# Gated slot attention and fp8 feed-forward: keys times queries with tokens in partitions, softmax weights turned by VectorE and DRAM

## The chip, the cores and the metric

The kernel runs on one core of a Trainium2 chip. The metric is the device time of one execution in microseconds (us). TensorE (PE in the profile) multiplies matrices; its weight loads are shown apart as PEld. VectorE (DVE), ScalarE (ACT) and GpSimd (POOL) work on vectors, and SyncE (SP) issues the DMAs. Each engine takes its instructions in program order and waits on semaphores that others raise.

## What is computed

Four batches of 512 tokens with 512 features go through a layer norm, an attention with 16 heads and 64 memory slots per head, a residual, another layer norm and a feed-forward with weights rounded to fp8. Cut to the attention's core, for every head:

```python
z = cumlogsumexp(s, axis=2); g = exp(shift(z) - z); p = exp(s - z)
hk = hk * g_t + k_t[..., None] * p_t          # 64 x 64 state, over tokens
ok = einsum('bhk,bhkm->bhm', q_t, hk)          # a number for each slot
pv = softmax(ok, axis=-1)                      # over the 64 slots
hv = hv * g_t[..., None] + p_t[..., None] * v_t
o  = einsum('bhm,bhmv->bhv', pv_t, hv)
o  = rms_norm(o) * silu(x @ Wg); y = o @ Wo
```

With e = exp(clip(s)) and c = the running sum of e over tokens, p and g fall out as quotients, so the kernel works with e, with 1/c ahead of the softmax and again behind it, and with plain causal products in chunks of 128 tokens.

## The kernel before

The attention is 32 **units**: a pair of heads (8 pairs) times a batch (4). Units 0 to 28 form the body, with i running 1 to 4 within a pair (unit 0 stands alone), units 29 to 31 the tail, which has the second layer norm beside it. Unit u works on its own scores while its projections ("jobs") for unit u+1 run between them: `ST` (slots), `KTJ` (keys), `QT` (queries), `VG0` to `VG3` (values and gates of a chunk), each 12 matmuls of 512 columns (L444 to L446). The order on every engine is written out by hand in `unit`; there is no scheduler.

TensorE in unit u: `ST`; the key states (L567) and, in one loop, the products of masked scores with e and of v with e (L580); `KTJ`; `ok` (L598, keys times queries, with slots in partitions); half of the output product of unit u-2; four transposes of p (L611), which put tokens in partitions for the softmax; the other half; `QT`; four transposes of the weights back (L620); `VG0`; the value weights (L633), the inter-chunk outputs (L638), the scores of u+1 (L505); `VG1`; the outputs (L650); `VG2`, `VG3`. Products are in fp32, so a logical matmul of the fp32 parts is two instructions in the trace. Up to unit 26 (`FAR`) the gated output is transposed by VectorE in blocks of 32x32 (`o_turn`) and by a DMA round trip through DRAM (`store_o`, `load_oT`); then `far_hi` (ScalarE) and `far_lo` (VectorE, L977 on oT_lo) split it in two parts for the output product, which waits for both (`s_oh`, `s_ol`). e and k of the next unit take the same kind of way: `e_turn`, `store_e`, `load_e` and `k_turn`, `store_k`, `load_k`. Before, a store is four DMAs that scatter 128 B pieces, and a load four DMAs of contiguous rows.

VectorE in unit u: `out_norm(u-1)` (L1093), `o_turn` (L1070), `clip` of the new slots (L988), `key_states` (L1030), `value_states` (L1040, L1043), `far_lo`, `e_turn` (L1056), where i = 3 the low parts of new weights (`lo_vg`, L977 on wvg_lo), the scaled ok (L1188), the softmax's maximum (L1202), subtraction (L1204) and sum (L1212), 1/c on the weights (L1226), `k_turn`, masks, and `sums` (L994 scan, L997 reciprocal) for u+1. ScalarE takes the exponential (L828). SP's queue holds all DMAs in one order.

Of the kernel before, what the change touches and what calls it, by code (L numbers as in the profile page):

```python
# [25 lines left out]
F32 = mybir.dt.float32  # L26
# [5 lines left out]
P = 128  # L32
# [4 lines left out]
CH = T // P  # L37
# [19 lines left out]
FAR = UNITS - B - 2  # L57

# [85 lines left out]
def attention(sb, sem, block, nc, x, Wq, Wk, Wv, Wg, Ws, Wo, gnorm, flat, gate_s, up_s, fp8_scratch, shared, ffn):  # L144
# [45 lines left out]
    ok_of = [pair_bank[:, c // 2, (c % 2) * P:(c % 2 + 1) * P] for c in range(CH)]  # L190
    hv_of = [pair_bank[:, c // 2, (2 + c % 2) * P:(3 + c % 2) * P] for c in range(CH - 1)]
    ok_both = pair_bank[:, :, 0:2 * P]
# [28 lines left out]
    s_eld, s_kld = sem("e_tok_loaded"), sem("k_tok_loaded")  # L221
    s_ob, s_ost, s_old = sem("o_blocks_turned"), sem("o_blocks_stored"), sem("oT_loaded")
# [3 lines left out]
    s_ok, s_oks, s_trs = sem("ok_done"), sem("ok_scaled"), sem("ok_transposed")  # L226
# [11 lines left out]
              k_read=s_kb, scores=s_a, e_read=s_hvd, weights_done=s_b, w_ready=s_wT, inter_done=s_oi,  # L238
# [21 lines left out]

    def product_of(u):

        if u > FAR + 1:
            return u - 1
        return u - 2 if u > 1 else None

    def o_free(eng, u):

        if u and u - 1 <= FAR:
            eng.wait_ge(s_ost, 16 * BL * u)  # L270
        elif u:
            eng.wait_ge(s_tro, 2 * (u - 1 - FAR))

# [19 lines left out]
    def _(sp):  # L293
# [50 lines left out]

        def store_o(v):

            sp.wait_ge(s_ob, v + 1)
            for i in range(BL):
                sp.dma_start(o_dram.rearrange("v b (n i t) -> i v (b n) t", i=BL, t=BK)[i],
                             o_flat[BK * i:BK * (i + 1), :].rearrange("v (n t) -> v n t", t=BK)).then_inc(s_ost, 16)  # L350

        def load_oT(v):

            sp.wait_ge(s_ost, 16 * BL * (v + 1))
            if v:
                sp.wait_ge(s_y, CH * v)
            for b in range(BL):
                sp.dma_start(ol[BK * b:BK * (b + 1), :, :].rearrange("v a t -> v (a t)").bitcast(F32), o_dram[:, b, :]
                             ).then_inc(s_old, 16)

        def store_e(nu):

            sp.wait_ge(s_eb, nu)
            for i in range(BL):
                sp.dma_start(e_dram.rearrange("t b (c i m) -> i t (b c) m", i=BL, m=BK)[i],
                             e_blocks[BK * i:BK * (i + 1), :].rearrange("t (n m) -> t n m", m=BK)
                             ).then_inc(s_est, 16)
# [1350 lines left out]
```

## Time and profile before

| | |
|---|---|
| time, median of 3 runs | 1384.22 us (1383.7 to 1384.83) |
| the profiled execution: its time, its span | 1384.27 us, 1382.6 us |
| TensorE busy, share of the span | 1357.9 us, 98% |
| VectorE busy | 1046.3 us, 76% |
| ScalarE, GpSimd busy | 401.0 us (29%), 138.4 us (10%) |
| packets of the DMA queue that SP issues | 307568, 32.8% of 16 engines' time |

The 1.7 us between the profiled execution's time and its span lie outside the instructions. Busy is what an engine spends inside its instructions; for TensorE the ends of matmuls are modelled and overlap. The rest of the section below are timelines, where a row gives start and duration of a group of like instructions and in brackets the idle time ahead of it.

### The profile page before, as it was taken

How to read it: one execution, taken by the hardware profiler on the slowest of the kernel's cores; microseconds unless marked ns; L12 is line 12 of the kernel's file. 1: busy time of each engine (PE TensorE's matmuls, PEld its weight loads, DVE VectorE, ACT ScalarE, POOL GpSimd, SP SyncE). 2: the span in 40 equal slices, each digit the busy share in tenths (PEclk: the TensorE clock that was granted, in tenths of full speed). 3: DMA queues.
4: the chain of work that ended last, by engine and by line, in shares of the span. 5: the costliest groups of instructions: out<-in, count | busy, mean ns of one | idle time of the engine just before them, and what ended most of it. 6: DMA issues, size and time to landing. Idle time of an engine off the chain costs nothing.

```text
span 1382.6 us, 21680 instructions
## 1 busy us (share of the span) xinstructions
PE 1357.9 (98%) x8047; PEld 1118.4 (81%) x8047; DVE 1046.3 (76%) x1650; ACT 401.0 (29%) x1181; POOL 138.4 (10%) x106
## 2 busy tenths in 40 slices
PE   6999999999999999999999999999999999999998
PEld 5788888888888888888888888888888878888886
DVE  8878878887888788778877887888778775535354
ACT  4322323332332233223322332233222323222221
POOL 3001101110110012001200110011010010000000
PEclk9999999999999999999999999999999999999999
DMA  6143334433533353335334433443121440000000
GB/s 183 45 124 92 86 84 123 98 87 82 129 90 83 82 130 87 87 84 136 89 84 96 114 86 86 106 113 81 41 81 28 134 122 1 31 1 30 0 31 31
DMA packets 307668, 113.99 MB, mean 82 GB/s; under 512 B 240496, under 2 KB 291312, under 8 KB 307568
## 3 DMA queue, kind: packets, MB, share of 16 engines
q1 hardware_dynamic: 307568, 112.67, 32.8%
q8 instruction: 62, 1.02, 0.3%
q14 instruction: 38, 0.31, 0.1%
HBM read 70.60 MB, written 42.01 MB: 81 GB/s over the span
## 4 chain that ended last, share of the span: by engine, by line
PE 93%; DVE 5%; issue 1%; DMA 1%; SPq 0%; POOL 0%; ACT 0%; DVEq 0%
PE bank L444 19%; PE bank L446 18%; PE bank L445 18%; PE bank L117 13%; PE bank L1563 6%; PE bank L650 4%; PE bank L580 4%; PE bank L633 3%; PE bank L505 2%; PE bank L567 2%; DVE wvg_lo L977 2%; PE bank L638 2%; PE bank L598 1%; PE bank L611 1%; PE bank L620 1%
## 5 line engine op out<-in xcount | busy, mean ns | idle before, releaser
L444 PE MATMUL bank<-wvg_hi,xT_hi 128*128 128x512 f32 x512 | 208.8, 408 | 0.0
L446 PE MATMUL bank<-wvg_hi,xT_lo 128*128 128x512 f32 x512 | 200.3, 391 | 0.0
L445 PE MATMUL bank<-wvg_lo,xT_hi 128*128 128x512 f32 x512 | 199.8, 390 | 0.0
L711 ACT ACTIVATE a_and_v<-bank 128x256 f32<-128x256 f32 x128 | 49.0, 382 | 286.3 <-PE bank L446 286.3
L1112 DVE TENSOR_TENSOR y<-y,bank 128x512 f32<-128x512 f32 x128 | 86.9, 684 | 49.4 <-PE bank L446 49.3
L444 PEld LDWEIGHTS bank<-wvg_hi,xT_hi 128*128 128x128 f32 x512 | 96.3, 188 | 21.5 <-issue 0.8
L446 PEld LDWEIGHTS bank<-wvg_hi,xT_lo 128*128 128x128 f32 x512 | 96.1, 188 | 21.0
L445 PEld LDWEIGHTS bank<-wvg_lo,xT_hi 128*128 128x128 f32 x512 | 96.5, 188 | 17.3
L997 DVE RECIPROCAL cT<-cT 128x512 f32<-128x512 f32 x32 | 107.3, 3354 | 1.1
L444 PE MATMUL bank<-wo_hi,oT_hi 128*128 128x512 f32 x256 | 105.9, 414 | 0.0
L949 POOL TENSOR_TENSOR rstd<-ssq,neg_half 128x8 f32<-128x8 f32 x32 | 52.3, 1636 | 491.1 <-DVE ssq L1049 491.1
L446 PE MATMUL bank<-wo_hi,oT_lo 128*128 128x512 f32 x256 | 100.6, 393 | 0.0
L445 PE MATMUL bank<-wo_lo,oT_hi 128*128 128x512 f32 x256 | 99.7, 389 | 0.0
L1002 DVE SCALAR_TENSOR_TENSOR g<-tanh_half_g,bank 128x256 f32<-128x256 f32 x128 | 51.7, 404 | 55.4 <-ACT tanh_half_g L761 55.4
L1433 DVE SCALAR_TENSOR_TENSOR gated<-gated,bank 128x512 f32<-128x512 f32 x48 | 32.9, 686 | 59.0 <-ACT gated L1422 59.0
L1563 PE MATMUL bank<-w_down,fuse_hi 128*128 128x512 f32 x192 | 74.8, 389 | 1.4 <-DVE fuse_lo L1448 1.4
L1563 PE MATMUL bank<-w_down,fuse_lo 128*128 128x512 f32 x192 | 74.7, 389 | 0.0
L828 ACT ACTIVATE p<-p 128x512 f32<-128x512 f32 x32 | 20.2, 633 | 159.9 <-DVE p L1204 159.9
L796 ACT ACTIVATE bank<-bank 128x128 f32<-128x128 f32 x236 | 64.6, 274 | 3.6 <-PE bank L650 3.0
L650 PEld LDWEIGHTS bank<-a_and_v 128*128 128x128 f32 x512 | 62.0, 191 | 2.5
L1429 ACT ACTIVATE fuse_hi<-gated 128x512 fp32r<-128x512 f32 x48 | 30.3, 632 | 110.3 <-DVE gated L1442 110.3
L650 PE MATMUL bank<-a_and_v 128*128 128x128 f32 x512 | 62.2, 275 | 0.0
(162 smaller groups left out, 3040.4 us busy)
## 6 DMA issues: line engine op xcount, KB each, us to landing
o_transposed<-o SPq DMA_DIRECT2D x108, 128.0 KB, 2.7
oT_lo<-o_transposed SPq DMA_DIRECT2D x108, 128.0 KB, 2.7
fp_weights<-q SPq DMA_DIRECT2D x28, 318.0 KB, 2.6
e_tokens<-k_tok_then_wT SPq DMA_DIRECT2D x124, 64.0 KB, 2.2
e_tok<-e_tokens SPq DMA_DIRECT2D x124, 64.0 KB, 2.0
k_tokens<-p SPq DMA_DIRECT2D x124, 48.0 KB, 2.1
k_tok_then_wT<-k_tokens SPq DMA_DIRECT2D x124, 48.0 KB, 1.9
stage_vg<-in_L_attn_Wv SPq DMA_DIRECT2D x32, 128.0 KB, 2.7
```

The costliest lines, as they stand in the source:

```text
L117: mm = pe.matmul(dst[:, :], w[:, k, at:at + P], part[:, k, bass.ds(b * T, T)], start=(k == 0 and part is xh), stop=(k == KT - 1 and part i ...
L444: pe.matmul(dst, w_hi, m_hi, start=(k == 0), stop=False)
L445: pe.matmul(dst, w_hi, m_lo, start=False, stop=False)
L446: last = pe.matmul(dst, w_lo, m_hi, start=False, stop=(k == n - 1))
L580: mm = pe.matmul(dst, e_tok[:, c, at], av[par][:, a, c, 0:both, :], start=(c % 2 == 0), stop=(c == 0), skip_group_check=True)
L650: mm = pe.matmul(O[a][:, c * P:(c + 1) * P], av[par][:, a, c, 0, :], av[par][:, a, c, 1, :], start=False, stop=(c == CH - 1), skip_group_c ...
L796: act.activation(unused, head, ACT.Square, accum_out=ssq[:, 2 * c + a:2 * c + a + 1]).then_inc(s_sq, 1)
L949: pool.tensor_tensor(rstd[:, :], ssq[:, :], neg_half[:, :], ALU.pow).then_inc(s_rstd, 1)
L997: dve.reciprocal(cT[i % 2][:, :], cT[i % 2][:, :]).then_inc(s_cinv, 1)
L1002: dve.scalar_tensor_tensor(out=g[i % 2][:, c, :, :].rearrange("p a d -> p (a d)"), in0=th[:, :], scalar=1.0, in1=job_bank(VGS[c], i)[:, 2 ...
L1112: dve.tensor_tensor(y[:, t, :], y[:, t, :], out_bank(u, c)[:, :], ALU.add).then_inc(s_ya, 1)
L1563: mm = pe.matmul(Y[c][:, :], part[f % 4][:, c * P:(c + 1) * P], wd, start=(f == 0 and part is ffn.fh), stop=(f == FT - 1 and part is ffn.fl))
```

## The change

Keys times queries swaps its operands: qT is now the stationary and hk the moving one, so `ok` comes out with tokens in partitions, and the four transposes L611 go in all units. The part of it within a chunk (a half of the old L580 loop) becomes 16 matmuls of 64 columns, the values' part 6 matmuls of 128. 1/c must now have tokens in partitions too: it is turned by VectorE (`c_sum`), stored and loaded by DMA as `c_tok`. Behind the exponential the weights are multiplied by `c_tok` in place, and in units 2 to 28 (`W_FAR`) they are turned by VectorE (`w_turn`), stored and loaded by DMA into wT; in the other five units TensorE still transposes them and ScalarE copies them (`wT_evac`). Unit 0 adds four transposes for its first c. All stores become one DMA with pieces of 512 B, all loads four DMAs that gather pieces of 128 B. The value product moves behind `VG1`, and VectorE's order changes. The key states' bank becomes `A[0]` up to unit 27.

```diff
+W_FAR = range(2, UNITS - B + 1)
 # DMAs
+        def store_blocks(dram, tile, signal):
+            sp.dma_start(dram.rearrange("c p f -> p c f"), tile.rearrange("p (c f) -> p c f", f=P)).then_inc(signal, 16)
+        def load_blocks(tile, dram, signal):
+            n = dram.shape[0] * BL
+            for b in range(BL):
+                sp.dma_start(tile[BK * b:BK * (b + 1), :].rearrange("t (n m) -> t n m", n=n),
+                             dram.rearrange("c (i t) f -> t (c i) f", t=BK)[:, :, BK * b:BK * (b + 1)]
+                             ).then_inc(signal, 16)
+        def load_c(nu):
+            sp.wait_ge(s_cst, 16 * nu)
+            sp.wait_ge(s_wm, nu)
+            load_blocks(c_tok, c_dram, s_cld)
+        def store_w(u):
+            sp.wait_ge(s_wb, far_before(u) + 1)
+            store_blocks(w_dram, p[:, :], s_wst)
+        def load_w(u):
+            sp.wait_ge(s_wst, 16 * (far_before(u) + 1))
+            load_blocks(wT[:, :], w_dram, s_wld)
             store_e(u + 1)
-            load_e(u + 1)
             if i == 1:
                 load_vg(pair)
+            if u in W_FAR:
+                store_w(u)
+            load_e(u + 1)
+            if u in W_FAR:
+                load_w(u)
 # TensorE
             for c in range(CH):
                 for a in range(2):
+                    at = slice(M * a, M * (a + 1))
+                    for h in range(2):
+                        ts = slice(64 * h, 64 * (h + 1))
+                        pe.matmul(ok_of[c][ts, at], av[par][:, a, c, 0, ts], e_tok[:, c, at],
+                                  start=(c == 0 and a == 0), stop=(c == 0), skip_group_check=True)
+            for c in range(CH - 1):
+                for a in range(2):
-                    mm = pe.matmul(dst, e_tok[:, c, at], av[par][:, a, c, 0:both, :],
-                                   start=(c % 2 == 0), stop=(c == 0), skip_group_check=True)
+                    mm = pe.matmul(hv_of[c][hs, :], e_tok[:, c, at], av[par][:, a, c, 1, :],
+                                   start=(c == 0), stop=(c == 0), skip_group_check=True)
-            pe.wait_ge(s_hv, 3 * (u + 1))
             for c in range(1, CH):
-                mm = pe.matmul(ok_of[c], hk[:, c - 1, :], qT[:, c * P:(c + 1) * P],
+                mm = pe.matmul(ok_of[c], qT[:, c * P:(c + 1) * P], hk[:, c - 1, :],
                                start=False, stop=True, skip_group_check=True)
             mm.then_inc(s_ok, 1)
+            if not first:
+                pe.wait_ge(s_oev, 2 * u)
-                out_product(v, (0, 1))
-            pe.wait_ge(s_oks, u + 1)
-            for c in range(CH):
-                mm = pe.transpose(T0[:, c * P:(c + 1) * P], p[:, c * P:(c + 1) * P], ident[:, :])
-            mm.then_inc(s_trs, 1)
-            if v is not None:
-                out_product(v, (2, 3))
+                out_product(v, range(CH))
+            pe.wait_ge(s_hv, 3 * (u + 1))
+            if u not in W_FAR:
+                w_transposes(u)
-            pe.wait_ge(s_exp, u + 1)
-            for c in range(CH):
-                mm = pe.transpose(T1[:, c * P:(c + 1) * P], p[:, c * P:(c + 1) * P], ident[:, :])
-            mm.then_inc(s_trw, 1)
                 job(VG0, nu, ni)
+                job(VG1, nu, ni)
-            pe.wait_ge(s_wT, u + 1)
+            if u in W_FAR:
+                pe.wait_ge(s_wld, 16 * BL * (far_before(u) + 1))
+            else:
+                pe.wait_ge(s_wT, near_before(u) + 1)
 # VectorE
+            dve.scalar_tensor_tensor(out=p[:, :], in0=T0[:, :], scalar=SCALE, in1=c_tok,
+                                     op0=ALU.mult, op1=ALU.mult).then_inc(s_oks, 1)
+            dve.tensor_tensor(p[:, :], p[:, :], c_tok, ALU.mult).then_inc(s_wm, 1)
+            if u in W_FAR:
+                w_turn(u)          # waits s_wm; dve.transpose(p, p) -> s_wb
             if not last:
                 k_turn(nu)
+                sums(nu, ni)       # scan, reciprocal, and for u > 0: dve.transpose(c_sum, c_sum) -> s_cb
                 gate(0, nu, ni)
+                gate(1, nu, ni)
             mask_value_weights(u, i)
```

What stands in VectorE's queue from a unit's start to the weights, unit 14, before (L1093 is `out_norm`, L1070 `o_turn`, L977 `far_lo`, L1056 `e_turn`, L1188 the scaled ok):

```order
L1093 TENSOR_TENSOR o<-o,rstd 128x4x128 x2
L1070 STREAM_TRANSPOSE o<-o 128x1024
L988 TENSOR_SCALAR eT<-bank 128x512
L1030 COPY hk<-bank 64x3x64 x2
L1040 COPY hv<-bank 128x128
L1043 TENSOR_TENSOR hv<-bank,hv 128x128 x2
L977 TENSOR_TENSOR oT_lo<-oT_lo,oT_hi 128x512 x2
L1056 STREAM_TRANSPOSE k_tok_then_wT<-eT 128x512
L1188 SCALAR_TENSOR_TENSOR p<-bank,cT 128x512
```

The same place in the changed kernel:

```order
L1062 TENSOR_SCALAR eT<-bank 128x512
L1111 COPY hk<-bank 64x3x64 x2
L1173 TENSOR_TENSOR o<-o,rstd 128x512 x2
L1121 COPY hv<-bank 128x128
L1124 TENSOR_TENSOR hv<-bank,hv 128x128 x2
L1156 STREAM_TRANSPOSE o<-o 128x1024
L1051 TENSOR_TENSOR oT_lo<-oT_lo,oT_hi 128x512 x2
L1264 SCALAR_TENSOR_TENSOR p<-bank,cT 128x512
L1267 TENSOR_REDUCE slot_max<-p 128x8
L1269 TENSOR_TENSOR p<-p,slot_max 128x512
```

The norm and the turn of the last unit's output have moved from ahead of the clip to behind the key and value states, and so stand directly ahead of `far_lo`; `e_turn` has moved behind the subtraction.

SP's queue in a unit with i = 4, before (after the loads of q, from the store of o on):

```order
L349 DMA o_transposed<-o 1024x1x32 x4
L365 DMA e_tokens<-k_tok_then_wT 512x1x32 x4
L374 DMA e_tok<-e_tokens 32x512 x4
L358 DMA oT_lo<-o_transposed 32x1024 x4
L381 DMA k_tokens<-p 384x1x32 x4
L390 DMA k_tok_then_wT<-k_tokens 32x384 x4
```

And in the changed kernel:

```order
L364 DMA o_transposed<-o 128x8x128
L364 DMA e_tokens<-k_tok_then_wT 128x4x128
L364 DMA w_slots<-p 128x4x128
L370 DMA e_tok<-e_tokens 32x16x32 x4
L370 DMA k_tok_then_wT<-w_slots 32x16x32 x4
L370 DMA oT_lo<-o_transposed 32x32x32 x4
L364 DMA k_tokens<-p 128x3x128
L364 DMA c_tokens<-cT 128x4x128
L370 DMA k_tok_then_wT<-k_tokens 32x12x32 x4
L370 DMA cT<-c_tokens 32x16x32 x4
```

The round trips of the weights (w_slots) and of 1/c (c_tokens) are new, and the load of e stands between the store and the load of the weights.

## Rows read from the trace of the kernel before

**Rows 1.** The page: DMA packets of the whole span.
```profile
DMA packets 307668, 113.99 MB, mean 82 GB/s; under 512 B 240496, under 2 KB 291312, under 8 KB 307568
```

**Rows 2.** Windows of units 14 and 15: length; PE, PEld, DVE, ACT, POOL busy; clock; DMA share, GB/s.
```profile
505.27:538.66 33.39, 33.39 (x212) 27.57 (x210) 27.75 (x42) 9.93 (x33) 5.53 (x5) 1.00 0.40 95
538.66:572.65 33.99, 33.61 (x212) 27.50 (x211) 29.36 (x44) 10.55 (x34) 4.62 (x4) 1.00 0.37 86
```

**Rows 3.** Timeline of TensorE in unit 14: start us, duration us.
```profile
505.27 0.39 PE L444 MATMUL bank<-xT_hi,ws_hi 128*128 128x512 f32 x1
...
508.79 1.69 PE L580 MATMUL bank<-a_and_v,e_tok 128*64 128x256 f32 x16
...
513.85 0.48 PE L444 MATMUL bank<-wo_hi,oT_hi 128*128 128x512 f32 x1
...
516.47 0.39 PE L446 MATMUL bank<-wo_hi,oT_lo 128*128 128x512 f32 x1
516.70 0.60 PE L611 MATMUL bank<-ident,p 128*128 128x128 f32 x4
...
517.37 0.39 PE L445 MATMUL bank<-wo_lo,oT_hi 128*128 128x512 f32 x1
...
525.91 1.16 PE L633 MATMUL bank<-k_tok_then_wT,eT 64*128 64x128 f32 x16
```

**Rows 4.** Timeline, both queues of TensorE, at 508.75 to 508.8 us.
```profile
508.68 0.14 PEld L567 LDWEIGHTS bank<-e_tok,k_tok_then_wT 128*64 128x64 f32 x2
508.74 0.20 PEld L580 LDWEIGHTS bank<-a_and_v,e_tok 128*64 128x64 f32 x3
```

**Rows 5.** Timeline of VectorE in unit 14.
```profile
506.50 1.29 DVE L1093 TENSOR_TENSOR o<-o,rstd 128x512 f32<-128x512 f32 x2
507.82 1.25 DVE L1070 STREAM_TRANSPOSE o<-o 128x1024 f32<-128x1024 f32 x1
508.99 0.65 DVE L988 TENSOR_SCALAR eT<-bank 128x512 f32<-128x512 f32 x1
509.57 0.72 DVE L1030 COPY hk<-bank 64x192 f32<-64x192 f32 x2
510.53 0.29 DVE L1040 COPY hv<-bank 128x128 f32<-128x128 f32 x1 [0.23 <-PE bank L580]
...
513.28 0.70 DVE L1056 STREAM_TRANSPOSE k_tok_then_wT<-eT 128x512 f32<-128x512 f32 x1
514.13 0.69 DVE L1188 SCALAR_TENSOR_TENSOR p<-bank,cT 128x512 f32<-128x512 f32 x1
...
517.51 0.68 DVE L1202 TENSOR_REDUCE slot_max<-bank 128x8 f32<-128x512 f32 x1
...
531.14 3.35 DVE L997 RECIPROCAL cT<-cT 128x512 f32<-128x512 f32 x1
```

**Rows 6.** Timeline of ScalarE: the softmax's exponential in unit 14.
```profile
518.95 0.63 ACT L828 ACTIVATE p<-p 128x512 f32<-128x512 f32 x1 [4.89 <-DVE p L1204]
```

**Rows 7.** Timelines of VectorE and TensorE in unit 15.
```profile
544.77 1.28 DVE L977 TENSOR_TENSOR oT_lo<-oT_lo,oT_hi 128x512 fp32r<-128x512 f32 x2
...
546.60 3.37 DVE L977 TENSOR_TENSOR wvg_lo<-stage_vg,wvg_hi 128x512 fp32r<-128x512 f32 x2
...
550.63 0.66 PE L611 MATMUL bank<-ident,p 128*128 128x128 f32 x4 [0.38 <-DVE p L1188]
```

**Rows 8.** Timeline of SyncE, which issues the DMAs, in unit 14.
```profile
503.86 0.38 SPq L342 DMA_DIRECT2D fp_weights<-q  x1
...
514.01 2.56 SPq L365 DMA_DIRECT2D e_tokens<-k_tok_then_wT  x4
```

**Rows 9.** The page, DMA issues: KB each, us to landing.
```profile
fp_weights<-q SPq DMA_DIRECT2D x28, 318.0 KB, 2.6
e_tokens<-k_tok_then_wT SPq DMA_DIRECT2D x124, 64.0 KB, 2.2
e_tok<-e_tokens SPq DMA_DIRECT2D x124, 64.0 KB, 2.0
```

More of the change, by code:

```diff
@@ L259, in splits_wait, with far_before, near_before, hk_bank @@
         return CH * (u if u > FAR + 1 else u - 1)
+    def far_before(u):
+        return max(0, min(u, W_FAR.stop) - W_FAR.start)
+    def near_before(u):
+        return u - far_before(u)
+    def hk_bank(u):
+        return A[0] if u <= FAR + 1 else O[0]
     def product_of(u):
@@ L514, in out_transposes, with w_transposes @@
                 mm.then_inc(s_tro, 1)
+        def w_transposes(u):
+            pe.wait_ge(s_wm, u + 1)
+            for c in range(CH):
+                mm = pe.transpose(T1[:, c * P:(c + 1) * P], p[:, c * P:(c + 1) * P], ident[:, :])
+            mm.then_inc(s_trw, 1)
         def out_product(u, chunks):
@@ L642, in unit @@
                 scores(nu)
-                job(VG1, nu, ni)
+                job(VG2, nu, ni)
             else:
@@ L826, in unit @@
                 evac(KTJ, nu, ni)
+            if first:
+                act.wait_ge(s_trc, 1)
+                copy(c_tok, A[1][:, :]).then_inc(s_ctok, 1)
             act.wait_ge(s_sub, u + 1)
             act.activation(p[:, :], p[:, :], ACT.Exp).then_inc(s_exp, 1)
+            if u not in W_FAR and product_of(u) is not None:
+                wT_evac(u)
             if last:
@@ L847, in unit @@
                 split_next_w(2, nu, ni)
+            if not last:
+                evac(VG2, nu, ni)
             head_squares(u, 0)
@@ L850, in unit @@
                 norm_hi(i - 1, (0, 1))
-            if not last:
-                evac(VG2, nu, ni)
             head_squares(u, 1)
@@ L1161, in unit @@
                 norm_lo(i - 2, (2, 3))
-            if not first:
-                out_norm(u - 1)
-            if u and u - 1 <= FAR:
-                o_turn(u - 1)
+            if not last:
+                clip(nu, ni)
             if u == FAR + 2:
@@ L1168, in unit @@
                     add_y(FAR, c)
-            if not last:
-                clip(nu, ni)
             key_states(u)
+            if not first:
+                out_norm(u - 1)
             value_states(u)
+            if u and u - 1 <= FAR:
+                o_turn(u - 1)
             if u > FAR + 1:
@@ L1176, in unit @@
                 far_lo(u - 2)
-            if not last:
-                e_turn(nu, ni)
             if i == 3 and not tail:
@@ L1241, in unit @@
                 return
[L1242 to L1243 removed]
+            if not tail:
+                quantise(u, slice(2, 4))
+            mask_scores(nu, ni)
             if tail:
                 norm_tokens(i - 1, (0, 1))
[L1246 to L1248 removed]
+            gate(2, nu, ni)
             times_gate(u, i, 1)
[L1250 removed]
             if not tail:
                 quantise(u, slice(4, Q8_STEPS))
+            times_gate(u, i, 0)
             if tail:
@@ L1255, in unit @@
                 norm_tokens(i - 1, (2, 3))
-            if not last:
-                gate(2, nu, ni)
-                mean_square(u)
-                gate(3, nu, ni)
+            mean_square(u)
+            gate(3, nu, ni)
             if u == FAR + 1:
```

206 lines of the change are left out of this document (102 added, 104 removed).

## The prediction

> **What bounds the kernel now.** I read the busy time by unit first: in unit 14 TensorE is busy for all of 33.39 us, at the full clock (1.00, 2.4 GHz), VectorE for 27.75 [rows 2]. Then TensorE's timeline of the same unit: groups follow one another without a gap, and 512-column matmuls start every 0.227 us [rows 3]. So a body unit ends when TensorE's list ends, and only TensorE's time, or a wait put into its list, moves the end. VectorE's timeline shows what such waits would hang on: it is 83% busy, in order, and feeds both the output product and the softmax [rows 5]. Units with i = 3 are the exception: unit 15 takes 33.99 us [rows 2], since two low parts of new weights (3.37 us) stand ahead of the scaled ok, and L611 waits 0.38 us for it [rows 7]. The sum starts from the profiled execution's own 1384.27 us, of which the span is 1382.6; the median of the runs, 1384.22, is the same number for this purpose.
>
> **1. Transposes that go.** From the last matmul start ahead of L611 (516.47) to the second behind it (517.37) are 0.90 us [rows 3]; two normal steps are 0.45, so a set of four costs 0.45. L611 goes in 32 units, L620 in 27, unit 0 gets one new set for c: 58 x 0.45 = 26.1 us. The i = 3 stall goes with L611: 7 x (33.99 - 33.39) = 4.2 us [rows 2]. Floor if nothing new waits: 1384.3 - 30.3 = 1354.0.
>
> **2. The new key product.** Before, the within-chunk part of ok was 8 of the 14 column sets of L580; now it is 16 matmuls of 64 outputs and 64 columns, in pairs on the two halves of the columns of the array. The number of columns streamed is the same; the number of weight loads doubles. Is a load of 64 outputs hidden under 64 columns? The nearest row is the last step of L567, 64 outputs and 64 columns as well: two loads start at 508.68 and the next two at 508.74 [rows 4], 0.06 us for a pair with its matmuls, which is what 64 fp32 columns cost (128 columns go in 0.11). So I take 0 for it; 32 instructions at that step are 0.85 us. The trace shows the step for four instructions only, so the other bound is that loads stop hiding: as much again, +0.85 us a unit, 27 us in all. The Trainium skill's page TensorE: Matmul & The Clock Gate, section "What overlaps and what doesn't" under Part 3, says that weight loads overlap matmuls in flight only when the row group differs. All 128 rows are used here, so by that rule the sum would be the 27 us worse. The step above speaks against it.
>
> **3. The output product waits for far_lo.** Times from the unit's start. TensorE ends ok at 513.85 - 505.27 = 8.58 us [rows 3], as before, since nothing ahead of it changes length. VectorE now: clip can start at 2.9 (ST is 12 x 0.227 = 2.7 long) and takes 0.58 to the next issue; key_states needs L567, which ends at 3.5, starts at 3.7 and takes 0.64; out_norm 1.2 more ends its issue at 5.56, so value_states starts then and not at 5.26 as in unit 14; value_states takes 0.86, o_turn 1.17 [rows 5], so far_lo starts at 7.6 and is done 1.28 later [rows 7], at 8.87. TensorE wants it at 8.58 and starts at 8.93; the 0.06 between is my allowance for the signal, about what separates 517.51 + 0.68 from its follower's chain of two steps in 1.44 [rows 5, 6]. That is 0.35 us in each of 26 units: 9.1 us. Before, the norm and the turn of o stood ahead of the clip, in the time of ST. In the i = 2 units GpSimd splits weights just then; I add 0.35 for these 7: 2.5 us.
>
> **4. The softmax chain and the weights' way through DRAM.** The scaled ok starts at 8.85 (in unit 14 at 514.13 - 505.27 [rows 5]). From there each dependent step of VectorE or ScalarE takes 0.72 or less (maximum at 517.51 to exponential at 518.95 is 1.44 for two [rows 5, 6]): scale, maximum, subtraction 2.15; exponential 0.66 [rows 6]; sum, product with c, turn (0.70 like L1056 [rows 5]) 2.13. The turn ends at 13.8. The store is one DMA with runs of 512 B, nearest to fp_weights<-q: 0.38 us of issue [rows 8], 2.6 to landing [rows 9]; meanwhile SP issues the four loads of e, which cost 0.38 to 0.64 each (single DMA; e's scattered ones, 2.56 for four [rows 8]). I take the dear end, since 512 pieces of 128 B are the same on the other side. The loads of the weights start at 16.7, the last is issued 1.9 later and lands after 2.0 to 2.2 [rows 9]: 20.9. TensorE wants them after the whole output product, QT, VG0 and VG1: 525.91 - 513.85 less two transpose sets plus 2.73 is 13.9 [rows 3], from 8.93 on, 22.8. Slack 1.9 us where i is 2 or 4: hidden, cost 0. If a load of scattered pieces took 2 us longer there would be nothing left: that is the cover's end.
>
> Where i = 3, the two low parts stand ahead of the scaled ok: 7.6 + 1.2 + 3.3 = 12.1, all else follows, the weights land at 24.1 or so: 1.3 us late, 7 x 1.3 = 9.1 us. Should they land sooner there, VectorE is the next limit: k_turn, scan, the reciprocal (3.35 [rows 5]) and the turn of c now stand ahead of gate 0, which VG2 needs, at 26.2 against VG2's 26.1 without a wait. Where i = 1, eight DMAs of new weights (8 x 0.4, by the 0.38 of [rows 8]) are issued ahead of the weights' store, which then leaves at 15.2 and not 13.8, and share the queue: 0.3 x 6 = 1.8 us.
>
> The turn of c is stored and loaded with all of VG2 to ok of the next unit as cover; k's load now waits behind the store of c, at 24.7, lands by 29.5, and is wanted at 35. Both cost 0. VectorE gets two turns of 0.70 a unit, 27.75 to 29.2 of some 33 us [rows 2]; its idle time hides them.
>
> **5. Ends.** Units 0 and 1 have no output product as cover between ok and the weights' transposes: VectorE needs 4.5 us from ok, QT gives 2.8, so TensorE waits 1.7, against 1.0 that L611 waited for p there (0.28 + 0.69 from [rows 3, 5]): 2 x 0.7 = 1.4. In units 28 to 31 the norm stands behind key_states, which a=1 of the output transposes may meet by 0.2: nothing taken.
>
> Sum: 1354.0 + 9.1 + 2.5 + 9.1 + 1.8 + 1.4 = 1377.9, **1378 us**, 0.45% faster. It says that four fifths of the transposes' time comes back as waits.
>
> **The rivals.**
> A, the forecast, as above: chance 0.42, own range 1370 to 1381.
> B, the loads that gather 128 B from DRAM are slow, the other side. No row has one; e's contiguous loads take 2.0 us, its scattered stores 2.2 [rows 9]. Place: `s_wld` in front of the value product. It decides from 1.9 us over my 7.1 us for the round trip; each us beyond costs 27 us, and i = 3 pays from the first: with 2.5 us more (say 1.1 us an issue, twice four loads) it is 7 x 2.5 + 20 x 0.6 + 6 x 1.4 = 38, 1416; with 1.2 more 7 x 1.2 + 6 x 0.9 = 14, 1392. For it: packets rise from 307668 [rows 1] by some 6500 in each of 27 units, to about 480,000, on one queue. Against: the queue's share is 0.40 in unit 14 [rows 2]. Chance 0.27. The Trainium skill, DMA: Bandwidth & Descriptors, section "Why small descriptors are slow (HBM only)", gives a fixed cost per packet and so speaks for B; no run here has such a load yet.
> C, loads stop hiding in the key product (part 2): 1378 + 27 = 1405. The 0.06 us step [rows 4] is against it. Chance 0.06. It is what the rule of the Trainium skill's page TensorE: Matmul & The Clock Gate would bring.
> D, far_lo and the weights are in time after all (loads issue at 0.4, VectorE's queue is ahead of my walk): no waits but the ends, 1354 + 1.4 to 1363. Chance 0.10.
> E, waits a little longer than mine everywhere (0.2 us a unit: gate 0, far_lo, the landing at i = 1): 1382 to 1387. Chance 0.15.
>
> **How the numbers follow.** About 0.2%, 2.8 us, is what a measurement of this kernel tells from no change. A falls wholly or nearly so under 1381.4, and so does D: faster 0.51. E and the edges of A and B: same 0.17. B, C and the rest of E: slower 0.32. The range for 8 in 10 leaves out the long end of B, C and the best part of D: 1362 to 1397.
>
> **What would show it.** Right: no L611, TensorE's rows in a steady unit near 32.8 us, 34 where i = 3; a wait of 0.3 to 0.4 us ahead of the output product in each, released by VectorE's oT_lo; a wait on the DMA of k_tok_then_wT from w_slots of about 1.3 us only where i = 3; L633's group (the 64-column one) and L638's together no longer than L580's 1.62 us. Wrong: the DMA wait in every unit (B), the key product near 2.4 us (C), units at 32.5 without waits (D). Most likely to break it are the 7.1 us of the round trip and the 1.3 us at i = 3.

## The result

The changed kernel takes 1424.34 us (median of 4 runs, 1419.58 to 1425.65) against 1384.32 (1383.7 to 1384.83): the ratio is 1.0283, with a 95% interval of 1.027 to 1.0296. It is 2.8% slower. The prediction said 1378, 0.45% faster, with a range from 1362 to 1397. The profiled execution has a span of 1422.8 us, 1.8 below its own time, so the rows below speak for the run.

The page of the changed kernel: busy time, packets (as [rows 1]), the first group of the output product with the wait ahead of it, and DMA issues (as [rows 9]).

```profile
PE 1347.6 (95%) x8711; PEld 1121.2 (79%) x8711; DVE 1075.2 (76%) x1708; ACT 410.3 (29%) x1187; POOL 140.0 (10%) x106
...
DMA packets 500554, 144.49 MB, mean 102 GB/s; under 512 B 359648, under 2 KB 491616, under 8 KB 500448
...
L488 PE MATMUL bank<-wo_hi,oT_hi 128*128 128x512 f32 x256 | 102.3, 400 | 27.4 <-DVE oT_lo L1051 27.4
...
e_tokens<-k_tok_then_wT SPq DMA_DIRECT2D x31, 256.0 KB, 2.3
e_tok<-e_tokens SPq DMA_DIRECT2D x124, 64.0 KB, 2.4
...
w_slots<-p SPq DMA_DIRECT2D x27, 256.0 KB, 2.3
```

TensorE's share fell from 98% to 95%: it has waits now. The gathering loads of e land after 2.4 us (2.0 before), its single stores and those of the weights after 2.3. The new store of 1/c takes longer, 3.6 us on the page, and no wait of TensorE hangs on it. Where the waits are, the windows of units 13 to 16 (i = 1, 2, 3, 4) show: length, then busy time of PE, PEld, DVE, ACT, POOL, then granted clock, DMA share, GB/s, as [rows 2].

```profile
489.55:528.23 38.68, 34.78 (x231) 28.75 (x230) 27.82 (x46) 11.03 (x34) 4.21 (x4) 0.96 0.59 137
528.23:562.53 34.30, 32.75 (x231) 27.37 (x230) 28.77 (x44) 10.23 (x33) 5.98 (x4) 1.00 0.56 123
562.53:597.05 34.52, 32.75 (x231) 27.38 (x230) 30.30 (x48) 10.75 (x34) 4.60 (x3) 1.00 0.53 115
597.05:630.11 33.06, 32.72 (x231) 27.38 (x230) 27.73 (x46) 8.59 (x30) 1.64 (x1) 1.00 0.52 112
```

TensorE's own work is 32.7 us in three of them, 0.6 less than the 33.39 of [rows 2]. All four lose something to a wait; the i = 1 unit loses by far the most, and its clock is 0.96. Mean lengths over units 2 to 27, each from the unit's first matmul to the next unit's, worked out from the two traces:

| | i = 1 (6 units) | i = 2 (7) | i = 3 (7) | i = 4 (6) |
|---|---|---|---|---|
| before | 33.39 | 33.39 | 34.00 | 33.39 |
| changed | 38.65 | 34.30 | 34.59 | 33.07 |
| my steps gave | 33.1 | 33.2 | 34.1 | 32.8 |

Against the kernel before, i = 1 costs 6 x 5.26 = 31.5 us, i = 2 6.4, i = 3 4.1, i = 4 gives 2 back: that is the 40 us. Against my sum the miss of 46 us is 33 at i = 1, 8 at i = 2, 3 at i = 3 and 1.4 at i = 4. What was waited for, from the waits of the changed kernel (total us, times, longest; L488 is the output product, L711 the outputs, L694 the value weights' product with the softmax weights, L789 ScalarE's scaling of the output weights wo, L1146 `k_turn`):

```profile
PE bank L488 <- DVE oT_lo L1051: 27.4, 26, 1.8
PE bank L711 <- DVE a_and_v L1101: 14.7, 6, 3.4
PE bank L694 <- DMA k_tok_then_wT<-w_slots: 9.4, 7, 2.4
...
ACT stage L789 <- DMA stage<-in_L_attn_Wo: 58.5, 8, 9.5
DVE p L1146 <- DMA w_slots<-p: 20.7, 7, 4.6
```

### The profile page after: what moved, and what is told of

Its sections match the earlier page's. It is cut to its first block, busy times and chain, and to the rows that moved or that the text cites. A ratio compares the mean times of both kernels' runs of the same rounds, so it can differ in the third digit from the quotient of the medians.

```text
span 1422.8 us, 23069 instructions
## 1 busy us (share of the span) xinstructions
PE 1347.6 (95%) x8711; PEld 1121.2 (79%) x8711; DVE 1075.2 (76%) x1708; ACT 410.3 (29%) x1187; POOL 140.0 (10%) x106
## 2 busy tenths in 40 slices
DMA packets 500554, 144.49 MB, mean 102 GB/s; under 512 B 359648, under 2 KB 491616, under 8 KB 500448
## 4 chain that ended last, share of the span: by engine, by line
PE 73%; DVE 14%; SPq 4%; DMA 4%; issue 3%; ACT 1%; POOL 0%; DVEq 0%; ACTq 0%
PE bank L488 14%; PE bank L490 14%; PE bank L489 14%; PE bank L118 12%; PE bank L1632 6%; PE bank L711 4%; DVE o L1173 3%; DVE oT_lo L1051 3%; DVE o L1156 2%; DMA w_slots<-p 2%; PE bank L694 2%; SPq L335 2%; SPq L370 2%; PE bank L620 2%; PE bank L548 2%
## 5 line engine op out<-in xcount | busy, mean ns | idle before, releaser
L488 PE MATMUL bank<-wvg_hi,xT_hi 128*128 128x512 f32 x512 | 206.8, 404 | 0.1
L488 PE MATMUL bank<-wo_hi,oT_hi 128*128 128x512 f32 x256 | 102.3, 400 | 27.4 <-DVE oT_lo L1051 27.4
L1083 DVE SCALAR_TENSOR_TENSOR g<-tanh_half_g,bank 128x256 f32<-128x256 f32 x128 | 52.6, 411 | 84.1 <-ACT tanh_half_g L821 84.1
L488 PEld LDWEIGHTS bank<-wvg_hi,xT_hi 128*128 128x128 f32 x512 | 97.0, 189 | 22.7 <-issue 1.2
L490 PEld LDWEIGHTS bank<-wvg_hi,xT_lo 128*128 128x128 f32 x512 | 96.5, 189 | 20.6
L1188 DVE TENSOR_TENSOR y<-y,bank 128x512 f32<-128x512 f32 x128 | 81.9, 679 | 3.3 <-PE bank L490 3.3
L711 PE MATMUL bank<-a_and_v 128*128 128x128 f32 x512 | 67.3, 288 | 14.7 <-DVE a_and_v L1101 14.7
L711 PEld LDWEIGHTS bank<-a_and_v 128*128 128x128 f32 x512 | 65.7, 203 | 19.2 <-DVE a_and_v L1101 17.2
L488 PEld LDWEIGHTS bank<-wo_hi,oT_hi 128*128 128x128 f32 x256 | 48.0, 188 | 41.1 <-issue 32.1
L771 ACT ACTIVATE qT<-bank 128x512 f32<-128x512 f32 x32 | 19.1, 598 | 157.5 <-PE bank L490 157.5
```

The source lines that it names most:

```text
L488: pe.matmul(dst, w_hi, m_hi, start=(k == 0), stop=False)
L490: last = pe.matmul(dst, w_lo, m_hi, start=False, stop=(k == n - 1))
L711: mm = pe.matmul(O[a][:, c * P:(c + 1) * P], av[par][:, a, c, 0, :], av[par][:, a, c, 1, :], start=False, stop=(c == CH - 1), skip_group_c ...
L771: return act.activation(dst, src, ACT.Copy)
L1083: dve.scalar_tensor_tensor(out=g[i % 2][:, c, :, :].rearrange("p a d -> p (a d)"), in0=th[:, :], scalar=1.0, in1=job_bank(VGS[c], i)[:, 2 ...
L1188: dve.tensor_tensor(y[:, t, :], y[:, t, :], out_bank(u, c)[:, :], ALU.add).then_inc(s_ya, 1)
```

## How an i = 1 unit loses 5.6 us

Unit 13 starts at 489.55. Three engines have to be read together. First SyncE's timeline: issue time and duration.

```profile
501.77 1.32 SPq L335 DMA_DIRECT2D stage_vg<-in_L_attn_Wv  x1
...
505.99 0.43 SPq L335 DMA_DIRECT2D stage_vg<-in_L_attn_Wg  x1
506.46 0.43 SPq L364 DMA_DIRECT2D w_slots<-p  x1
506.99 2.29 SPq L370 DMA_DIRECT2D e_tok<-e_tokens  x4
509.74 1.90 SPq L370 DMA_DIRECT2D k_tok_then_wT<-w_slots  x4
511.74 2.73 SPq L370 DMA_DIRECT2D oT_lo<-o_transposed  x4
514.51 0.76 SPq L364 DMA_DIRECT2D k_tokens<-p  x1
515.32 0.48 SPq L341 DMA_DIRECT2D stage<-in_L_attn_Wo  x1
```

The eight loads of new weights hold the queue from 501.77 to 506.42, while the softmax weights are ready by 503.56. Everything behind them is late, and so is the second load of wo, far down the list at 515.32. Then VectorE.

```profile
502.85 0.71 DVE L1151 STREAM_TRANSPOSE p<-p 128x512 f32<-128x512 f32 x1
...
509.82 0.58 DVE L1146 STREAM_TRANSPOSE p<-kT 128x384 f32<-128x384 f32 x1 [2.89 <-DMA w_slots<-p]
...
520.88 0.42 DVE L1083 SCALAR_TENSOR_TENSOR g<-tanh_half_g,bank 128x256 f32<-128x256 f32 x1 [4.79 <-ACT tanh_half_g L821]
521.22 1.28 DVE L1101 TENSOR_TENSOR a_and_v<-bank,tri 128x512 f32<-128x512 f32 x2
```

`k_turn` (L1146) writes into p, the buffer that the weights are stored from, so it waits 2.89 us for that store. Gate 1 (L1083) waits another 4.79 us for a tanh, and the mask (L1101) stands behind gate 1. ScalarE says why the tanh is late.

```profile
510.26 0.38 ACT L821 ACTIVATE tanh_half_g<-bank 128x256 f32<-128x256 f32 x1
518.92 0.72 ACT L789 ACTIVATE stage<-stage,half_gn 128x512 f32<-128x512 f32 x1 [8.28 <-DMA stage<-in_L_attn_Wo]
519.67 0.63 ACT L771 ACTIVATE wo_hi<-stage 128x512 fp32r<-128x512 f32 x1
...
520.47 0.38 ACT L821 ACTIVATE tanh_half_g<-bank 128x256 f32<-128x256 f32 x1
```

In ScalarE's list the scaling of wo (L789) stands ahead of `VG1`'s tanh, and it waits 8.28 us for a load that was issued at 515.32. TensorE's timeline ends the chain: the softmax weights come 0.79 us late (L694), and the outputs (L711) wait 2.71 us for the mask.

```profile
513.45 1.16 PE L694 MATMUL bank<-k_tok_then_wT,eT 64*128 64x128 f32 x16 [0.79 <-DMA k_tok_then_wT<-w_slots]
...
521.96 3.10 PE L711 MATMUL bank<-a_and_v 128*128 128x128 f32 x16 [2.71 <-DVE a_and_v L1101]
524.71 0.77 PE L488 MATMUL bank<-wvg_hi,xT_hi 128*128 128x512 f32 x1
```

The kernel before has a wait at the same place on ScalarE, and nothing on TensorE hung on it, since gate 1 stood behind the mask and the sums. From its waits:

```profile
ACT stage L729 <- DMA stage<-in_L_attn_Wo: 36.2, 8, 5.3
```

L711 itself takes 3.10 us in unit 13, and 1.95 in a unit without the wait (unit 16). Windows of unit 13 show the granted clock (the number behind the five busy times) around the wait.

```profile
516.00:519.20 3.20, 3.14 (x16) 2.17 (x12) 0.09 (x1) 0.28 (x1) 0.00 (x0) 1.00 0.93 245
519.20:521.90 2.70, 0.04 (x1) 0.00 (x0) 1.02 (x3) 2.27 (x6) 1.27 (x1) 1.00 0.65 105
...
523.50:524.70 1.20, 1.20 (x8) 1.20 (x7) 1.20 (x3) 1.09 (x8) 0.00 (x0) 0.50 0.58 173
524.70:526.00 1.30, 1.30 (x5) 1.11 (x5) 1.30 (x3) 0.00 (x0) 0.00 (x0) 0.50 0.00 0
```

After 2.7 us in which TensorE had nothing to do, its clock was at 0.50, the 1.2 GHz level, until about 526, when it was already busy again. L711 lost 1.05 us to that and the job behind it 0.72. So unit 13 is 5.62 us above an i = 4 unit: 0.86 for the weights' DMA, 2.86 for the mask, 1.77 for the clock, 0.13 in L548. Over the span the mean clock is 0.993 against 0.999 before; (0.007 - 0.001) x 1422.8 is 8.5 us of the 40. The clock fell in five of the six i = 1 units.

Unit 13 is one of six, and the shares differ: the wait for the softmax weights is 0.79 to 2.37 us (mean 1.5), the wait for the mask 0.81 to 3.41 us (mean 2.45).

## The experiments

All times are medians against the kernel before in the same set of runs (1384.17 to 1384.35 us). The table gives, in each kernel's trace, when things happen in an i = 1 unit: means over the six units, in us from the unit's first matmul. It is worked out from the timelines.

| kernel | store of weights | load of wo | ScalarE scales wo | k_turn | mask | value weights on TensorE (L694) | outputs on TensorE (L711) | unit |
|---|---|---|---|---|---|---|---|---|
| changed | 16.5 | 26.1 | 30.0 | 20.7 | 32.3 | 24.6 | 33.0 | 38.65 |
| e1 | 14.0 | 27.6 | 30.9 | 17.3 | 33.2 | 23.0 | 34.0 | 40.99 |
| e2 | 16.5 | 25.8 | 29.5 | 20.6 | 26.8 | 24.4 | 30.0 | 35.54 |
| e3 | 16.5 | 25.1 | 29.2 | 20.6 | 31.5 | 24.4 | 32.2 | 37.12 |
| e10 | 14.0 | 22.5 | 26.1 | 17.3 | 28.4 | 23.0 | 29.1 | 33.79 |
| e7 | 14.0 | 21.8 | 25.4 | 17.3 | 27.7 | 23.1 | 28.7 | 33.29 |

**e1: the loads of new weights behind the load of the softmax weights.** On SyncE's list:

```diff
-            if i == 1:
-                load_vg(pair)
             if u in W_FAR:
                 store_w(u)
             load_e(u + 1)
             if u in W_FAR:
                 load_w(u)
+            if i == 1:
+                load_vg(pair)
             if u - 1 <= FAR:
                 load_oT(u - 1)
```

> Only SP's order changes: in units with i = 1 the eight loads of new weights (stage_vg) are issued behind the load of the softmax weights instead of ahead of their store. Theory A (the late store of the weights, 506.46 us instead of 503.6 in unit 13 of the changed kernel, is what makes the units with i = 1 5.6 us longer than those with i = 4): these six units fall from 38.7 to about 33.1 us, total about 1391 us. Theory B (the larger part, 4.6 us, comes over ScalarE: it waits for the output weights' load, issued behind store_k, before it can give VG1's tanh, gate 1 waits for that tanh, and the mask of the value weights, which L711 needs, now stands behind gate 1): the load of wo is issued as late as before, since the eight issues now stand ahead of load_oT; only the 0.8 us wait on the DMA goes, units with i = 1 at about 37.8 us, total about 1419 us.

Measured: 1436.83 us (1435.95 to 1438.12), ratio 1.038 (1.0362 to 1.0397), 12.5 us over the changed kernel. Neither theory's number came, 1391 or 1419: B took the load of wo to go out as late as before, and it went out later still. The table shows which cause acts: the weights now leave at 14.0 and TensorE has them on time (L694 at 23.0), `k_turn` is not held up either (17.3), and the unit is still the longest of all, because the load of wo went out 1.5 us later. In its waits the DMA of the weights is gone from TensorE and the mask costs twice as much:

```profile
PE bank L711 <- DVE a_and_v L1101: 31.6, 6, 6.1
```

So the softmax weights' own lateness is not what makes i = 1 long.

**e2: gate 1 behind the mask on VectorE,** the queue of SyncE as in the changed kernel.

```diff
                 gate(0, nu, ni)
-                gate(1, nu, ni)
             mask_value_weights(u, i)
+            if not last:
+                gate(1, nu, ni)
```

> Only VectorE's order changes: gate 1 goes behind the mask of the value weights (as it was in the kernel before, where it stood behind the sums too). Theory A (late store of the weights): the wait on the weights' DMA, 0.8 us, and what follows stay, units with i = 1 at 37.5 us or more, total 1418 or more. Theory B (gate 1 waits for ScalarE, which waits for wo's load): the waits of 2.9 and 1.0 us ahead of and inside L711 go, about 0.5 us may stay ahead of VG3, units with i = 1 at about 34.6 us, total about 1400 us. Neither expects anything in the other units.

Measured: 1406.14 us (1404.19 to 1407.43), ratio 1.0155 (1.0138 to 1.0172): 18 us back. The load of wo and ScalarE are as late as before (29.5), and the mask starts 5.5 us sooner. What is left at i = 1 is the weights' DMA (8.0 us in the waits of TensorE's L694) and a wait of up to 0.6 us for gate 1 itself. With the waits shorter the clock stays up: 0.999 over the span. This shows that the step from ScalarE to TensorE goes through gate 1. The units stay 0.9 us above theory B's 34.6 and the total 6 us above its 1400. The link before it, ScalarE's order, no run moved by itself. It rests on the row of 8.28 us and on the table: wherever gate 1 stands ahead of the mask (changed, e1, e3, e10, e7), the mask starts 2.3 us behind the scaling of wo, whenever that is.

**e5: the weights transposed by TensorE in all units,** so that nothing of them passes through DRAM.

```diff
-W_FAR = range(2, UNITS - B + 1)
+W_FAR = range(2, 2)
```

> The swapped key product, the turned c and all of the order stay; in units 2 to 28 the softmax weights too are transposed by TensorE and copied by ScalarE, not moved through DRAM. TensorE pays 27 x 0.45 = 12 us. If the round trip of the weights (late store, k_turn behind it, one queue for all DMAs) is behind the 5.6 us of the units with i = 1, these fall to about 33.5 us and the total is about 1424 - 6 x 5.2 - 20 x 0 + 12 - (what was saved already: 0) = 1405 us. If the units with i = 1 stay near 39 us, the cause is in the order of VectorE and ScalarE alone, and the total is about 1436 us.

Measured: 1405.24 us (1404.54 to 1406.82), ratio 1.015 (1.0133 to 1.0166). By i the units take 34.07, 34.76, 34.98 and 33.53. At i = 2 and i = 4 that is 0.46 us over the changed kernel: the four transposes, which I had priced at 0.45. At i = 1 it is 4.6 us under it: the store and four loads are gone from the queue, `k_turn` waits for no store, and the load of wo goes out at 22.7. In the changed kernel as it stands, the DMA way loses more at i = 1 (6 x 4.6 = 27) than it saves elsewhere (20 x 0.45 = 9).

**e4: far_lo directly behind the norm of o,** ahead of the value states and the turn of o.

```diff
             if not first:
                 out_norm(u - 1)
+            if 1 < u <= FAR + 1:
+                far_lo(u - 2)
             value_states(u)
...
-            elif u > 1:
-                far_lo(u - 2)
```

> Only VectorE's order changes: far_lo goes ahead of value_states and o_turn, directly behind out_norm. If the wait ahead of the output product (0.6 us where i is 1 or 4, 1.8 where i = 2, 2.0 where i = 3) is VectorE's queue, it goes in all 26 units: units with i = 4 from 33.06 to 32.5 us, i = 2 from 34.3 to 32.5, i = 3 from 34.5 to 32.5 plus what the softmax weights are then late (up to 1.4 us), total about 1424 - 26 x 0.6 - 7 x 1.2 - 7 x 0.6 = 1396 us. If the wait is ScalarE's (far_hi late behind weight splits where i is 2 or 3), only the 0.6 us of i = 1 and 4 goes and the total is about 1416 us.

Measured: 1394.5 us (1392.87 to 1396.77), ratio 1.0079 (1.0062 to 1.0096): 30 us back from an edit that moves one step past three. TensorE's wait for oT_lo, 27.4 us, is gone. The i = 4 units fall from 33.07 to 32.52, so the wait there costs 0.55 and not 0.35; i = 2 falls by 1.57, i = 3 by 1.72, i = 1 by 0.9.

**e7: the order of SyncE's list alone.** The loads of new weights go to the end of the unit's list, and the second load of wo ahead of the store of k.

```diff
-            if i == 1:
-                load_vg(pair)
...
                 load_oT(u - 1)
+            if u == UNITS - B or (i == 1 and u > 1):
+                load_o(u // B, 1)
             store_k(u + 1)
...
-            if u == UNITS - B or (i == 1 and u > 1):
-                load_o(u // B, 1)
...
             load_c(u + 1)
             if i == 1:
+                load_vg(pair)
                 load_skq(pair, 0)
```

> Only SP's order in units with i = 1: the eight loads of new weights go to the end of the unit's list, and the load of wo goes ahead of the store of k. The theory that stands after the first runs: what TensorE waits for there is the mask, behind gate 1, behind ScalarE's VG1 tanh, behind the load of wo (issued 25.8 us into the unit, landed 3.6 us later). With the load issued near 21 us and landed near 25 us, ScalarE is done before VG1's tanh delays the mask beyond L711: units with i = 1 fall from 38.7 to about 33.1 us, total about 1391 us, all other units unchanged. Rival: the time is lost to the 1 MB of new weights itself, which contends with the other DMAs wherever it stands; then units with i = 1 stay over 35 us and the total over 1403 us.

Measured: 1384.55 us (10 runs, 1383.77 to 1385.85), ratio 1.0005 (0.9996 to 1.0015): no difference from the kernel before, and all of the 40 us gone. The i = 1 units take 33.29, so the rival, that the new weights cost their time wherever they stand, falls. The surprise of some 7 us is at i = 2, 33.25 and not 34.30, and is told of below.

**e3 and e10: e7's two moves apart.** e3 moves only the load of wo, e10 only the loads of new weights.

> Only the second load of wo moves, from behind the store of k to ahead of it on SP's queue; new weights stay ahead of the store of the softmax weights. It can be issued about 0.5 to 0.8 us sooner (at 514.5 and not 515.3 in unit 13 of the changed kernel), since SP has no wait left there. If the i = 1 units are long because ScalarE waits in order for this load, ahead of gate 1: 0.7 x 6 = 4 us less than the changed kernel, 1420. If the store of k in front of it is what costs (a rival: SP itself stands in it waiting for k_turn): several us a unit, near 1400.

> Only the eight loads of new weights move, from ahead of the store of the softmax weights to the end of the unit's list on SP's queue; wo's load keeps its place behind the store of k. The weights' store leaves some 4 us sooner, so k_turn does not wait, and the load of wo goes out some 3 to 4 us sooner. Theory (position on SP's queue, reached through ScalarE's in-order wait): i = 1 units fall from 38.65 to 33.3 to 34.5 us, 1385 to 1392. Rival (wo's place behind the store of k holds a good part of the loss): i = 1 stays above 35.5, 1398 or more.

Measured: e3 1414.91 us (1413.16 to 1416.17), ratio 1.0222 (1.0205 to 1.0239); e10 1391.22 us (1389.5 to 1391.74), ratio 1.0048 (1.0031 to 1.0064). e10 alone brings 33 us, and lies in the range that the theory of the queue gave. e3 brings 9.4 us where 4 were expected. The outputs come 0.8 us sooner, as expected (5 us in all); and the mean clock rises from 0.993 to 0.996, worth 0.003 x 1413 = 4 us: a shorter wait leaves less time at the low clock. The rival, that SyncE stands at the store of k, would have given 24 us and falls.

**e9: VectorE makes all four low parts of new weights at i = 3, GpSimd none,** nothing else as against the changed kernel.

```diff
-            if i == 3 and not tail:                      # GpSimd
-                pool.wait_ge(s_job, job_count(VG3, u, i))
-                for k in range(2, KT):
-                    lo_vg(pair_of_next(u), k)
...
             if i == 3 and not tail:                      # VectorE
-                for k in range(2):
+                for k in range(KT):
                     lo_vg(pair_of_next(u), k)
```

> The changed kernel, but VectorE makes all four low parts of the new weights where i = 3 and GpSimd none. Theory: VectorE's far_lo takes 2.68 us instead of 1.25 there because GpSimd reads and writes SBUF at the same time, and this is why TensorE waits 2.0 us ahead of the output product instead of 0.6. Then the wait falls to about 0.6 and units with i = 3 from 34.5 to 33.1 us, plus up to 1 us if the two more low parts (1.3 us) make the softmax weights late: total 1424 - 7 x 1.4 = 1414 us, 1421 with the late weights. Rival: far_lo waits for ScalarE, which splits the same weights; then units with i = 3 stay at 34.5 us or rise.

Measured: 1416.42 us (1415.7 to 1417.34), ratio 1.0235 (1.0218 to 1.0252), 8 us under the changed kernel although VectorE does more; the i = 3 units fall from 34.59 to 33.62. VectorE at i = 3 in the changed kernel, with GpSimd's row ahead of the two of VectorE:

```profile
569.56 2.96 POOL L994 TENSOR_TENSOR wvg_lo<-stage_vg,wvg_hi 128x512 fp32r<-128x512 f32 x2 [5.22 <-ACT wvg_hi L771]
...
570.39 2.68 DVE L1051 TENSOR_TENSOR oT_lo<-oT_lo,oT_hi 128x512 fp32r<-128x512 f32 x2
572.99 1.28 DVE L1051 TENSOR_TENSOR wvg_lo<-stage_vg,wvg_hi 128x512 fp32r<-128x512 f32 x2
```

And in e9:

```profile
564.44 1.25 DVE L1047 TENSOR_TENSOR oT_lo<-oT_lo,oT_hi 128x512 fp32r<-128x512 f32 x2
565.61 2.49 DVE L1047 TENSOR_TENSOR wvg_lo<-stage_vg,wvg_hi 128x512 fp32r<-128x512 f32 x4
```

The same `far_lo` takes 2.68 us beside GpSimd and 1.25 without it. The rival, that it waits for ScalarE's splits, falls. Four low parts on VectorE take 2.49 us, less than the 3.37 that two took in [rows 7].

**e6, e8, e11: what the findings add up to.** e6 is e7 with e4's move of `far_lo`. e8 is e6 with gate 1 behind the mask, as in e2. e11 is e6 with VectorE making all low parts, as in e9.

> far_lo ahead of value_states and SP's new order of the units with i = 1, together. If the two causes are independent, body units come to 32.5 us (i = 1 and 4), 32.7 (i = 2) and 32.9 (i = 3): from the 1394.5 us with far_lo alone, six units fall from 37.75 to 32.6 us, total about 1363 us, 1.5% under the kernel before. If the round trip of the softmax weights is then late everywhere (it takes 6.9 us from the store's issue and was hidden behind the wait for far_lo), units would be 33 us and the total about 1375 us.

> As the run with far_lo and SP's order, and gate 1 behind the mask as well. If ScalarE's wait for wo's load is gone with SP's order, gate 1 is no longer late and this changes nothing: 1363 us within 2. If some of it is left, this is 3 to 8 us faster than that run. Risk: VG3 waits for gate 1, now 1.3 us later, which it can bear by 2 us.

> The kernel with far_lo ahead and the new order on SP's queue, and besides it VectorE makes all four low parts of new weights at i = 3, GpSimd none. In that kernel GpSimd's two take 2.54 us there, beside value_states, the turn of o and VectorE's own two (1.65 us). All four on VectorE took 2.49 us in the run that made them so, 0.85 more than 1.65. If VectorE's time ahead of the scaled ok decides: weights later by 0.85 us at i = 3, 7 x (0.5 to 0.85) = 3.5 to 6 us slower, 1370 to 1373. If what was left there was the sharing between the two engines: 1 to 2 us faster, 1365.

Measured: e6 1366.96 us (1364.44 to 1369.38), ratio 0.9883 (0.9866 to 0.9899); e8 1368.53 us (1367.73 to 1369.0), ratio 0.9886 (0.987 to 0.9903); e11 1371.26 us (1367.76 to 1371.37), ratio 0.9899 (0.9882 to 0.9915). e6 beats both kernels, the one before by 1.2% and the changed one by 4%, with no other change than the places of three steps. It is 4 us above the 1363 expected. Its trace is of its fastest execution (1364.44). Its windows of units 13 to 16:

```profile
464.38:496.92 32.54, 32.54 (x232) 27.30 (x231) 26.12 (x44) 10.21 (x29) 4.23 (x3) 1.00 0.60 132
496.92:530.03 33.11, 32.79 (x231) 27.36 (x230) 29.88 (x47) 11.07 (x39) 5.50 (x4) 1.00 0.67 157
530.03:563.22 33.19, 32.62 (x231) 27.30 (x230) 29.21 (x48) 10.76 (x34) 4.18 (x3) 1.00 0.54 119
563.22:595.80 32.58, 32.58 (x231) 27.30 (x230) 27.69 (x46) 8.67 (x30) 1.64 (x1) 1.00 0.53 114
```

Means by i are 32.88, 32.98, 32.73 and 32.53; 32.5 is a unit without any wait. e8 came neither to the 1363 nor 3 to 8 us under e6: it gains at i = 1 (32.52) and pays at i = 2 (33.82), so it is no better. Its load of the next ws (the slots' weights) comes late there, and ScalarE, in order, has the split of ws ahead of `oT_hi`, which `far_lo` needs. In its waits on TensorE:

```profile
PE bank L487 <- DVE oT_lo L1050: 6.3, 6, 1.5
```

It is the i = 1 mechanism once more, one unit later. Why e8's load lands later than e6's was not followed further. e11 lies in the 1370 to 1373 of its first theory, but its runs and e6's overlap, so the total alone settles little. The i = 3 units do: they pay 0.64 us, inside the 0.5 to 0.85 of that theory, since with `far_lo` already out of GpSimd's way VectorE's added work only makes the softmax weights later. The 0.4 at i = 2 is none of that; there ws_lo starts later than in e6 in five of the seven units (7.0 us into unit 14, for 6.35), as in e8.

## Why the prediction was wrong

**The step that failed is the i = 1 sentence of part 4**: "0.3 x 6 = 1.8 us". It priced the eight new-weight loads by what they do to the softmax weights, the store that leaves at 15.2. Even that was too small: the store leaves at 16.5, and TensorE waits 1.5 us for the weights on the mean. The runs put 5.3 us on the whole step (38.65 against 33.29 in e7), 32 us in all. Three things were missing: the second load of wo is queued behind all of them (e10, e7); ScalarE waits for it in order, ahead of the tanh (the 8.28 us row; e1, by the table); and the change had put gate 1, which needs the tanh, ahead of the mask, which TensorE needs (e2). I wrote down VectorE's new order and asked what stands behind `k_turn`, the scan and the reciprocal only as far as gate 0. That `k_turn` waits for the store out of p was not in my steps at all. The clock, 8.5 us, followed from the wait.

**Part 3, the output product waits for far_lo: right in kind, too small.** At i = 4 it is 0.55 (e4) for 0.35. At i = 2 it was to be 0.7 and is 1.57, at i = 3 0.35 and is 1.72 (both e4). The profile row at i = 3 reads:

```profile
573.21 0.47 PE L488 MATMUL bank<-wo_hi,oT_hi 128*128 128x512 f32 x1 [1.77 <-DVE oT_lo L1051]
```

The cause at i = 3 is GpSimd working at the same time, shown under e9. Before, GpSimd's low parts fell beside VectorE's own low parts, where nothing hung on them but the scaled ok: that is what 3.37 us for two instructions in [rows 7] says, when `far_lo`'s two take 1.28. I took 3.37 for the price of the step by itself. The change moved `far_lo` back into GpSimd's time. The Trainium skill, SBUF — State Buffer, section "Who interferes with whom", states it: a VectorE instruction with two inputs in SBUF and a GpSimd instruction that reads SBUF shut each other out for a whole instruction. The trace agrees: 1.25 became 2.68, near one GpSimd instruction (1.48) more. The turn of o beside the same instructions kept its 1.23 us.

At i = 2 it is `out_norm` that meets ws_lo, GpSimd's low part of ws. First the changed kernel, where ws_lo starts 4.9 us into unit 14, then e7, where it starts 6.3 us into it, since ws's load stands behind the eight loads of new weights:

```profile
532.74 2.40 DVE L1173 TENSOR_TENSOR o<-o,rstd 128x512 f32<-128x512 f32 x2
...
533.11 1.48 POOL L984 TENSOR_TENSOR ws_lo<-stage,ws_hi 128x512 fp32r<-128x512 f32 x1 [3.25 <-ACT ws_hi L771]
```

```profile
510.71 1.29 DVE L1172 TENSOR_TENSOR o<-o,rstd 128x512 f32<-128x512 f32 x2
...
512.52 1.30 POOL L983 TENSOR_TENSOR ws_lo<-stage,ws_hi 128x512 fp32r<-128x512 f32 x1 [3.50 <-ACT ws_hi L770]
```

With GpSimd past it, the norm takes 1.29 again. That is e7's surprise: 7 x 1.05 us at i = 2, won by a load that comes later. No run moved ws's load alone, but e10's seven i = 2 units show both cases in one execution: in three ws_lo starts at 5.2 or later, the norm takes 1.29 and the unit 33.2; in four it starts at 4.87 and the unit takes 34.3.

**Part 4 at i = 2 and 4: right, cost 0; at i = 3 the mechanism was wrong.** In unit 16 the store leaves 14.0 us into the unit and the loads start at 16.65, for my 13.8 and 16.7. In unit 14 they go at 543.37 and 546.47, some 1.4 us later than that, and nothing waits. At i = 3 I had the weights land at 24.1 and TensorE wait 1.3 us for them. They land 23.1 to 25.0 us into the unit, but TensorE, held up by the wait ahead of the output product, wants them only at 24.5, and it waits in one unit of seven, 0.5 us. Where that wait is gone (e4), TensorE is there at 22.5, and the weights are in time in four of the seven units: VectorE's own low parts take 1.28 us now and not 3.37. The price went to `far_lo` instead, and the unit is 34.59 for my 34.1. That this came out near is luck.

**Part 1: right.** A set of transposes costs 0.46 (e5), for 0.45; units without waits take 32.52 (e4, e6), for the 32.5 of rival D.

**Part 2: right, 0 taken.** The key product, in unit 14 of the changed kernel:

```profile
531.75 1.10 PE L633 MATMUL bank<-e_tok,a_and_v 128*64 128x64 f32 x32
532.69 0.83 PE L638 MATMUL bank<-a_and_v,e_tok 128*64 128x128 f32 x12
533.44 0.50 PE L488 MATMUL bank<-xT_hi,wk_hi 128*128 128x512 f32 x1
```

From the first start to L488's are 1.69 us, 0.08 more than the loop that it replaces, so rival C falls. The rule of the Trainium skill's page TensorE: Matmul & The Clock Gate, section "What overlaps and what doesn't" under Part 3, by which I had estimated 0.85 more, is not borne out here.

**Part 5** came within 1.5 us: unit 0 is 1.0 longer, unit 1 0.5, the tail 1.4 shorter.

**Rival B**, slow gathering loads, gave times near the measured one (1416) and is refuted all the same: they land after 2.3 to 2.4 us, issue takes 0.5 each, and TensorE waits for them nowhere at i = 2 or 4 and once, 0.5 us, at i = 3. The packets, 500554, are as many as it feared. Rival D's 1355 to 1363 are what the change can bring when nothing is late; e6 comes within 4 us of that.

## What to carry to other kernels

When a change puts DMAs into an in-order queue, list every load behind them, and for each the engine that waits for it in order, and what stands behind that wait; the transfer that the change is about may be the harmless one. When a step is moved on VectorE, look at what GpSimd does in its new place: an instruction that takes twice its usual time in the trace, like `far_lo` here, may be telling of the engine beside it and not of its own size. And a reordering belongs to the change: here the same arithmetic was 4% faster with three steps in other places.

## What was not expected of the hardware

In unit 13 a wait of 2.7 us on TensorE cost 1.8 us more through the clock at 1.2 GHz, which lasted until some 4 us after the wait's end. It does not always fall: unit 21, with waits of 1.48 and 2.39 us, kept the full clock and is the shortest of the six at 37.27 us, and in unit 25 the clock fell after a wait of 1.86. One of the four runs of the changed kernel had a mean clock of 0.998 and took 1419.58 us, the others 0.992 to 0.993 and 1424.1 to 1425.7; only one of the latter was profiled, so the waits of the fast one are not known. And the first of the eight weight loads in unit 13 took 1.32 us to issue where the others took 0.43; why was not tried.
